# Expert results scattered to token rows as they come, read back by plain loads, with three shared tiles between the batches

## What is computed

```
nx = rmsnorm(X, g2); logits = nx @ Wr.T + expert_bias
topw, topi = top_k(softmax(logits), 2); topw = softmax(topw)
shared = swiglu(nx, sW1, sW2, sW3)
eo[e] = (silu(nx @ eW1[e].T) * (nx @ eW3[e].T)) @ eW2[e].T      # 8 experts, 256 wide
out = x + gb * (X + shared + sum over the two chosen experts of topw * eo)
```

## Time and profile before

| | us |
|---|---|
| median of 3 timed runs (1410.04 to 1413.48) | 1412.84 |
| the profiled execution, its own time | 1408.02 |
| its span, first to last instruction | 1405.9 |
| TensorE busy, share of the span | 1262.6 (90%) |
| VectorE busy | 1083.5 (77%) |
| ScalarE busy | 877.1 (62%) |
| GpSimd busy | 412.5 (29%) |
| mean granted TensorE clock | 0.966 of full |

### The profile page before, as it was taken

The page is one execution under the profiler, slowest core; times in us unless marked ns, Lnnn a source line. Parts: engine busy times, 40 slices in busy tenths (PEclk is TensorE's granted clock), DMA queues, the critical chain, the costliest instruction groups (busy, mean ns, idle before and its releaser), DMA issues.

```text
span 1405.9 us, 18718 instructions
## 1 busy us (share of the span) xinstructions
PE 1262.6 (90%) x5880; PEld 901.4 (64%) x5880; DVE 1083.5 (77%) x2304; ACT 877.1 (62%) x1399; POOL 412.5 (29%) x440
## 2 busy tenths in 40 slices
PE   3975768999999999999999999989997979989985
PEld 2434545666667666767756766656556868778874
DVE  4867768888988888888978887899755786557756
ACT  2645756767878667767797776657577634334431
POOL 0156421112211112201113211115631355853234
PEclk9988879999999999999999999999999989999998
DMA  5001036000000000000000002002212536645445
GB/s 203 8 1 60 1 120 239 9 5 5 9 4 9 4 5 5 8 5 5 8 4 9 23 12 86 16 5 79 83 53 95 172 117 192 203 136 153 146 136 162
DMA packets 64893, 91.22 MB, mean 65 GB/s; under 512 B 12703, under 2 KB 52704, under 8 KB 64544
## 3 DMA queue, kind: packets, MB, share of 16 engines
q1 hardware_dynamic: 45662, 55.27, 11.9%
q0 software_dynamic: 13920, 31.40, 8.1%
q10 hardware_dynamic: 5218, 3.39, 0.8%
HBM read 48.15 MB, written 41.80 MB: 64 GB/s over the span
## 4 chain that ended last, share of the span: by engine, by line
PE 65%; DVE 13%; ACT 8%; issue 6%; POOL 4%; DMA 2%; ACTq 1%; another core or an unknown queue 1%; POOLq 0%; DVEq 0%
PE PS L1982 10%; PE PS L1905 7%; PE PS L1908 6%; PE PS L1922 6%; PE PS L1925 6%; PE PS L1923 6%; PE PS L1857 6%; PE PS L2012 5%; DVE mx L1226 4%; DVE PL L1272 3%; PE PS L1843 2%; PE PS L1966 2%; POOL xbuf L1645 2%; PE PS L1995 1%; PE PS L1870 1%
## 5 line engine op out<-in xcount | busy, mean ns | idle before, releaser
L1226 DVE TENSOR_REDUCE mx<-PS 128x1 f32<-128x512 f32 x512 | 344.3, 684 | 48.3 <-PE PS L1857 47.2
L845 ACT ACTIVATE PT<-PS 128x1024 f32<-128x1024 f32 x256 | 262.3, 1025 | 188.6 <-PE PS L1908 182.5
L1272 DVE TENSOR_TENSOR PL<-PT,PH 128x512 fp32r<-128x512 f32 x512 | 358.7, 708 | 16.3 <-ACT PH L848 15.0
L848 ACT ACTIVATE PH<-PT 128x1024 fp32r<-128x1024 f32 x256 | 271.5, 1060 | 8.1
L1922 PE MATMUL PS<-PH,VH 128*65 128x512 f32 x512 | 213.2, 416 | 2.2 <-ACT OZ L859 2.0
L1925 PE MATMUL PS<-PL,VH 128*65 128x512 f32 x512 | 202.7, 396 | 0.0
L1923 PE MATMUL PS<-PH,VL 128*65 128x512 f32 x512 | 202.4, 395 | 0.0
L1857 PE MATMUL PS<-KA,Q 128*128 128x512 f32 x384 | 154.3, 411 | 13.5 <-DVE mx L1226 9.4
L1905 PE MATMUL PS<-Q,KA 128*128 128x512 f32 x384 | 129.8, 420 | 2.9 <-DMA Q<-mT 2.9
L1908 PE MATMUL PS<-Q,KB 65*128 65x512 f32 x384 | 122.0, 399 | 0.0
L950 ACT ACTIVATE sg<-PS 128x256 f32<-128x256 f32 x110 | 42.2, 383 | 103.0 <-PE PS L1982 86.5
(11 more groups left out here) (268 smaller groups left out, 2543.3 us busy)
## 6 DMA issues: line engine op xcount, KB each, us to landing
xbuf<-xT SPq DMA_DIRECT2D x26, 384.0 KB, 4.5
nxT<-in_wexp SPq DMA_DIRECT2D x9, 768.0 KB, 4.5
xg<-xbuf SPq DMA_DIRECT2D x52, 128.0 KB
ybuf<-nxT SPq DMA_DIRECT2D x44, 128.0 KB
ybuf<-yo SPq DMA_DIRECT2D x34, 128.0 KB
x<-in_x SPq DMA_DIRECT2D x8, 512.0 KB, 12.1
x_scratch<-x SPq DMA_DIRECT2D x2, 2048.0 KB, 7.3
nxT<-norm_scratch POOLq DMA_DIRECT2D x32, 128.0 KB
```

The source lines that it names most:

```text
L845: act.activation(PT[:, gs % 4, :], PS[:, bk:bk + 2, :].rearrange("p a n -> p (a n)"), ACT.Exp, scale=0.125).then_inc(sem("pt"), 1)
L848: act.activation(PH[:, gs % 4, :], PT[:, gs % 4, :], ACT.Copy).then_inc(sem("pt_h"), 1)
L1226: dve.tensor_reduce(mx[:, qb % 2, i, c:c + 1], PS[:, k, :], AX, ALU.max).then_inc(sem("dve_out"), 1)
L1272: dve.tensor_tensor(PL[:, gs % 4, cols], PT[:, gs % 4, cols], phf[:, gs % 4, cols], ALU.subtract).then_inc(sem("pl"), 1)
```

## The change

What a tile of experts computes is now sent straight to token order. A new buffer `ytok` in HBM has two rows of 256 per token of both batches, and behind them as many rows as there are expert rows, for those that belong to no token. So that a tile knows where its rows go, each row of `xbuf` gets two numbers more (`DR` = 258): the code is filled by a list (`nowhere`) for all rows, and `scatter` overwrites it with the token's own (`hdr`) for the rows in use. Per expert tile VectorE makes 128 row numbers `yi` from the two numbers and the tile's expert, and GpSimd stores the result with one indirect DMA, where SyncE had a plain one. `gather` becomes a plain load on SyncE's queue, 16 in all, each of two groups of 128 tokens with both rows; `y12` is now two places of twice the size. The batch 1 `scatter_load` goes to SyncE's queue. Three of the 16 closing shared tiles are moved between the batches, and the side jobs get other steps. The rows of `xbuf` are no longer contiguous for the zeroing DMAs, and a DMA of 4992 pieces of 8 bytes is added behind each batch's zeros. `NEARLY` is 3 and `FIRST` 97.

The order:

```
-TILES = ([(None, NT + i) for i in range(NT)] + [(0, i) for i in range(NTI)] + [(1, i) for i in range(NTI)]
-         + [(None, i) for i in range(NT)])
+TILES = ([(None, NT + i) for i in range(NT)] + [(0, i) for i in range(NTI)] + [(None, i) for i in range(NEARLY)]
+         + [(1, i) for i in range(NTI)]
+         + [(None, i) for i in range(NEARLY, NT)])
...
-            (20, 1, total_jobs(0)),
+            (17, 1, total_jobs(0)),
             (17, 1, route_jobs(1, 4)),
-            (30, 3, scatter_jobs(1)),
-            (50, 1, total_jobs(1)),
-            (NT + NTI + 3, 0.5, gather_jobs(0)),
-            (NT + NTI + 8, 0.5, finish_jobs(0)),
-            (NT + 2 * NTI + 1, 1, gather_jobs(1)),
-            (NT + 2 * NTI + 5, 1, finish_jobs(1))]
+            (30, 2.4, scatter_jobs(1)),
+            (56, 0.5, total_jobs(1)),
+            (NT + NTI + 9, 0.25, gather_jobs(0)),
+            (NT + NTI + 13, 0.5, finish_jobs(0)),
+            (FIRST + 2, 1, gather_jobs(1)),
+            (FIRST + 4, 2, finish_jobs(1))]
```

On SyncE:

```
+        def gather(h):
+            b, i, r = h // 8, h % 8, h % NYQ
+            for k in range(NYO):
+                w.wait_ge(sem(f"d_y{k}"), 16 * stored(b, k))
...
+            if h >= NYQ:
+                w.wait_ge(sem("comb"), 2 * (h - NYQ) + 2)
+            src = ytok[2 * b * S:2 * b * S + 2 * S, :].rearrange("(p t j) d -> p t j d", p=P, t=NT)
+            sp.dma_start(yq[:, r, :, :, :], src[:, 2 * i:2 * i + 2, :, :]).then_inc(sem(f"d_yq{r}"), 16)
...
+        def scatter_load(b, i):
+            n, r = b * NT + i, (b * NT + i) % NSX
+            if b:
+                w.wait_ge(*kept(token(b, i)))
+                w.wait_ge(sem(f"d_sx{r}"), 32 * (n // NSX))
+                sp.dma_start(sx[:, r, 0:D], nrm[b, i]).then_inc(sem(f"d_sm{r}"), 16)
...
             for n in range(NTI // 3):
-                sp.dma_start(zv[n], bc(zero, 3, 1)).then_inc(sem("d_zero"), 16)
+                sp.dma_start(rows_of[n][:, :, 0:D], bc(zero, 3, 1)).then_inc(sem("d_zero"), 16)
+            sp.dma_start(xbuf[b][:, D:DR], I["nowhere"][b]).then_inc(sem("d_zero"), 16)
```

On ScalarE's queue, at the start:

```
-        act.dma_start(thr[:, :], I["thr"]).then_inc(sem("d_route"), 16)
+        act.dma_start(thr[:, :], I["thr"].to_broadcast([P, NTI])).then_inc(sem("d_route"), 16)
+        act.dma_start(hdr[:, :, :, :], I["codes"]).then_inc(sem("d_route"), 16)
```

On VectorE, in the chooser, the placer and behind the split of tile `s`:

```
+                    mark(dve.tensor_scalar(hdr[:, b, :, 0], rm[:, 4, :], -1.0, float(NE), ALU.mult, ALU.add))
...
+            dve.tensor_scalar(texpf[:, b, :], r_v[:, :], float(NE - 1), None, ALU.min).then_inc(sem("texp"), 1)
...
+                dve.scalar_tensor_tensor(yi[:, k % NYI:k % NYI + 1], xr[r][:, D:D + 1], texpf[:, g, i:i + 1],
+                                         xr[r][:, D + 1:DR], ALU.not_equal, ALU.add).then_inc(sem("yi"), 1)
```

On GpSimd, in `scatter`, and a store per expert tile at the head of each step:

```
+            pool.tensor_copy(sx[:, r, D:DR], hdr[:, b, i, :]).then_inc(sem("sx"), 1)
+            w.wait_ge(sem("sx"), n + 1)
...
+        def store(s):
+            k, r = nth[s], nth[s] % NYO
+            w.wait_ge(sem("yo"), k + 1)
+            w.wait_ge(sem("yi"), k + 1)
+            pool.indirect_dma_start(
+                out=ytok, out_offset=bass.IndirectOffsetOnAxis(ap=yi[:, k % NYI:k % NYI + 1], axis=0),
+                in_=yr[r], in_offset=None).then_inc(sem(f"d_y{r}"), 16)
```

More of the change, by code:

```diff
@@ L29 @@
 NYO = 7
+NYI = 16
+NYQ = 2
+NEARLY = 3
+DR = D + 2
 def bc(ap, n, axis):
@@ L158, in gather_jobs @@
 def gather_jobs(b):
-    return [("gather", b * NT + i) for i in range(NT)]
+    return [("gather", b * NT // 2 + i) for i in range(NT // 2)]
 def finish_jobs(b):
@@ L309, in _build @@
     x1d = nc.dram_tensor("x1_scratch", [NB, S, D], F32, kind="Internal").ap()
-    xbuf = [nc.dram_tensor(f"xbuf{b}", [NTI * P, D], F32, kind="Internal").ap() for b in range(NB)]
-    ybuf = [nc.dram_tensor(f"ybuf{b}", [NTI * P, D], F32, kind="Internal").ap() for b in range(NB)]
+    xbuf = [nc.dram_tensor(f"xbuf{b}", [NTI * P, DR], F32, kind="Internal").ap() for b in range(NB)]
+    ytok = nc.dram_tensor("ytok", [2 * NB * (S + NTI * P), D], F32, kind="Internal").ap()
     tri = sb("tri", [P, 2, P])
@@ L434, in _build @@
     wl = sb("wl", [P, NE, 2, 768], F32R)
+    xg2 = sb("xg2", [P, NXR - 4, DR])
+    xr = [xg[:, i, :] for i in range(4)] + [xg2[:, i, :] for i in range(NXR - 4)]
+    yq = y12[:, :, :, :].rearrange("p (r t) j d -> p r t j d", r=NYQ)
     xhf = xh[:, :, :, :].bitcast(F32)
     hhf = hh[:, :, :, :].bitcast(F32)
-    sx = nxT[:, 1, 1024:2048].rearrange("p (s d) -> p s d", d=D)
+    w0 = W[0][:, :, :, :].rearrange("p a c n -> p (a c n)")
+    sx = w0[:, 3072:3072 + NSX * DR].rearrange("p (s d) -> p s d", d=DR)
     wst = nxT[:, :, :].rearrange("p c n -> p (c n)")[:, 0:4 * 768].rearrange("p (s c n) -> p s c n", s=2, c=2)
@@ L631, in fetch @@
             m = s - NT
-            experts_free(w)
-            keys_free(w)
-            pe_of(w, ("proj_last", NT - 1, 0))
+            attention_done(w)
             if m >= NXR:
                 w.wait_ge(sem("tx"), s - NXR + 1)
+                if TILES[s - NXR][0] is not None:
+                    w.wait_ge(sem("yi"), nth[s - NXR] + 1)
             if g is None:
@@ L681, in _ @@
         work = {"spill": spill, "max_turn": max_turn, "load_w": load_w, "split_down": split_down, "finish": finish,
-                "rescale": rescale}
+                "rescale": rescale, "gather": gather, "scatter_load": scatter_load}
         run(work, FRONT)
@@ L1685, in split_down @@
                                ALU.subtract).then_inc(sem("w_down"), 1)
-        def gather(n):
-            b, i, s = n // NT, n % NT, n % NG
-            experts_free(w)
-            for r in range(NYO):
-                w.wait_ge(sem(f"d_y{r}"), 16 * stored(b, r))
-            w.wait_ge(sem("w2h"), 1)
-            w.wait_ge(sem("w2l"), 1)
-            w.wait_ge(sem("tx"), NT)
-            for m in range(token(1, NT - 6), token(1, NT)):
-                w.wait_ge(*kept(m))
-            if n >= NG:
-                w.wait_ge(sem("comb"), n - NG + 1)
-            for j in range(2):
-                pool.indirect_dma_start(
-                    out=y12[:, s, j, :], out_offset=None, in_=ybuf[b],
-                    in_offset=bass.IndirectOffsetOnAxis(ap=slot[:, b, j, i:i + 1], axis=0)).then_inc(sem(f"d_pair{s}"), 16)
+        def store(s):
+            g, i = TILES[s]
+            if g is None:
+                return
+            k, r = nth[s], nth[s] % NYO
[4 more added lines that the diff above has]
+                in_=yr[r], in_offset=None).then_inc(sem(f"d_y{r}"), 16)
         after_last("zero")
@@ L1711, in _ @@
                 "q_hi": q_hi, "z_out": z_out, "z_back": z_back, "scatter": scatter, "split_down": split_down,
[L1712 removed]
+                "rl_scale": rl_scale, "scatter_load": scatter_load, "t_mul": t_mul, "t_add": t_add}
         run(work, FRONT)
@@ L1719, in _ @@
                 run(work, LOOP[gs, part])
-        for s in range(-3, NTL + 3):
+        run(work, TAIL[-3])
+        for s in range(-2, NTL + 2):
+            if 0 <= s - 2 < NTL:
+                store(s - 2)
             run(work, TAIL[s])
+        run(work, TAIL[NTL + 2])
     @block.tensor
@@ L2073 @@
     wol[:64, :D], wol[64, D] = tr(a["L0_ffn_Wo"])[3 * 64:], 1.0
+    token = 16 * np.arange(P)[:, None, None] + np.arange(16)[None, None, :] + 2048 * np.arange(2)[None, :, None]
+    codes = np.stack([np.zeros(token.shape), 2 * token], axis=3).astype(np.float32)
+    nowhere = np.zeros((2, NTI * P, 2), np.float32)
+    nowhere[:, :, 1] = 2 * 4096 + 2 * np.arange(2 * NTI * P).reshape(2, NTI * P)
     arrays = {
@@ L2082 @@
         "thr": (np.arange(NTI) * P).astype(np.float32).reshape(1, NTI), "mask": mask,
+        "codes": codes, "nowhere": nowhere,
         "pri": np.arange(NE, 0, -1).astype(np.float32),
```

97 lines of the change are left out of this document (56 added, 41 removed).

## The result

The changed kernel takes 1464.77 us (median of 4 runs, 1461.71 to 1466.31) against 1413.16 (4 runs): ratio 1.0369, 95% interval 1.0351 to 1.0387. It is slower by 51.6 us; 1409.8 was forecast, with 1394 to 1429 as the range. The profiled execution has a span of 1459.5 us, 53.6 more than before.

The account below looks back on a forecast made before the run. It took TensorE to bound the kernel outside three holes beside dense indirect DMAs, with the gathers last at the end. Terms -9.7 - 15.3 + 5 + 3 + 0.5 + 1 + 11 + 0.5 + 1 = -3.0 gave 1409.8 us, range 1394 to 1429.

Parts of the forecast that it names:

- GpSimd's queue in the batch 1 scatters: Before the first batch 1 tile: result stores between scatters delay the last scatter; TensorE's 6.0 hole becomes about 9, +3 us.
- Zeros and lists: SyncE's queue ahead of the row of maxima near 238: lists 10.6, zero rows 2, less 1.6 slack, +11 us.
- The last attention block: Before the attention's end: sixteen copies in GpSimd's queue, where projection already waits now and then, +1 us.
- the holes beside the gathers: Expert tiles beside gathers: TensorE's holes go if dense indirect DMAs make them, -15.3 us; otherwise nothing.
- two finishes in a step: Closing tiles: VectorE's step with two finishes takes 3.15 us, over TensorE's 2.54, for eight steps, +5 us.
- the end: After the last tile's start: plain loads replace gathers, leaving 9.3 us of that tile's own chain instead of 19.0, -9.7 us.
- routing and passes: Batch 1 routing and later passes: an added small VectorE operation per tile can meet GpSimd's passes, +0.5 and +1 us.
- the front: Start of the kernel: two more loads ahead on ACT's queue, +0.5 us.
- Rival 1: Front and routing: lists ride inside the slack and routing gets its relief, 9 and 4.5 us better, 1396; chance 0.33.
- Rival 2: Eighth step of the attention loop: lists cost as much per piece as whole rows, 18 us worse, 1428; chance 0.11.
- Rival 3: Expert tiles: the holes aren't the gathers' doing and stay, 15 us worse, 1425; chance 0.13.
- Rival 4: Batch 1 routing: VectorE's code operation is caught behind GpSimd's passes, 2.0 us each, eight times, 15 us worse, 1425; chance 0.11.

Follow-up runs that it names:

- e4: Changed kernel with the batch 1 token loads back on GpSimd, one plain DMA ahead of each pair of scatters: 1446.9 us, single execution.
- e5: Changed kernel with one plain GpSimd DMA of 8 bytes behind each pair of batch 1 scatters: 1441.3 us, single execution.
- h1: Token order for batch 1 alone, batch 0 keeping plain stores and gathers, three shared tiles between batches: 1409.8 us (kernel before beside it: 1406.3).
- e6: Changed kernel with a GpSimd memset of 128x512 behind each pair of batch 1 scatters: 1451.6 us, single execution.
- e8: Changed kernel without the 32 GpSimd copies of codes; one DMA per batch writes them behind the kept rows: 1450.8 us, single execution.
- e9: Changed kernel with a plain GpSimd DMA of 8 bytes behind every second pair of batch 1 scatters only: 1448.9 us, single execution.
- e3: Changed kernel with zeros and lists issued one at every second attention step from step 12: 1437.9 us, single execution.
- e1: Changed kernel with both lists issued at attention steps 12 and 20, behind the row of maxima; zeros stay in place: 1445.0 us, single execution.
- e2: Changed kernel with zeroing DMAs writing whole rows of 258 numbers, no lists, and result stores skipping rows without a token: 1446.0 us, single execution.
- e7: Kernel before with one plain GpSimd DMA of 8 bytes behind each pair of gathers, 32 in all: 1407.8 us, single execution.
- e10: Kernel before with a GpSimd memset of 0.54 us behind each pair of gathers: 1398.9 us in a single execution; timed again, ratio 0.9928.

## Why the prediction was wrong, step by step

**The step that failed** is "GpSimd's queue in the batch 1 scatters", +3, with 6 less to 16 more as its bounds; it measured **+25.6**. It went wrong twice. The first error: the prediction had read that the holes of before stand beside dense indirect DMAs, took 15.3 us off for that, and then filled the batch 1 scatters with 49 indirect DMAs where there were 32, with the loads that had spaced them taken away, and charged only their time on the queue. It put nothing down for new holes. e4 and e5, which space the same DMAs again, take 92.4 and 93.2 us for tiles 30 to 58 instead of 102.6, so the holes are some 10 us of the 25.6.

The second error was in the queue time itself, and by e4 and e5 it is the other 15. The last scatter was put 67.6 us after 1168.85, as if the first could start as early as before. It started 10.1 us after tile 30 instead of 3.7, because stores that wait for their results stand ahead of it, and the last one ends 84.1 us after tile 30 instead of 53.9. In the changed kernel pauses of over 0.6 us in GpSimd's queue add up to 11.4 us on the way, against 2.2 before; but e4 has no such pause, does the loads as well, and ends at 83.8. With the stores of batch 0 out of this queue (h1) the last scatter ends at 57.4, and the whole loss is gone. The wait of 6.4 us for the first batch 1 tile never came in the changed kernel, since TensorE arrived later than the data; e4, with few holes, shows it at 12.5.

**Zeros and lists**, +11, measured 28.5 in the profiled run. The place was right (SyncE's queue ahead of the row for the ninth step) and so was the lack of slack. The zeros were mis-sized: 2 us with 7 as their upper end, measured 10.5. In the six profiled kernels with the lists ahead of the row (after, e4, e5, e6, e8, e9) the delay at step 10, less what was there at step 3, is 19.9 to 28.5, median 21.9 (e3, with nothing ahead of the row, shows 1.6 by the same count). Less the 10.5 of e1, the lists cost 9.4 to 18.0, median 11.4, or 18 ns a piece, where 10.6 and 17 ns were taken, and the execution of the changed kernel that stands here is the dearest of the six.

What the trace shows is 26 DMAs of the same 1 KB pieces in 34.1 us at a pitch of 1032 bytes and in 28.9 at 1024, 18% more; the row behind them lands 4 us later after its issue as well.

The Trainium skill, DMA: Bandwidth & Descriptors, How a descriptor splits into AXI transactions, says of reads that a transaction covers at most 256 bytes and has to start at a multiple of 256, so that a piece which starts elsewhere begins with a partly used one. For 1 KB that makes five transactions instead of four; an estimate by their number is up to 25% more, 36 us. e1 (34.1) and e2 (36.0) agree in size, but these are writes, and no run here shows the transactions themselves.

The prediction also weighed a rule of the same page of the Trainium skill (Specifications), that pieces below 512 bytes are read, modified and written; by its estimate the lists would cost 14.2 us at least. The 9.4 to 18.0 measured, with 11.4 as the median, do not decide that.

**The last attention block**, +1, measured 9.2, some 5 of it the copies (e8). The copies were priced by their duration, but each stands in the queue of the four small DMAs that the projection waits for. In the changed kernel TensorE waits 6.64 and 3.77 us there, where the kernel before waits 2.83 and 0.83, and e8 4.22 and 2.74:

```profile
1023.47 0.37 PE L1916 MATMUL PS<-ident,m 128*4 128x128 f32 x1 [6.64 <-DVE m L1263]
...
1067.21 1.22 PE L1923 MATMUL PS<-woa,O 128*128 128x256 f32 x2 [3.77 <-POOL O L1671]
```

**Right in mechanism and size:** the holes beside the gathers, -15.3 (tiles 58 to 109: -7.9, after the finishes' 4.5 and two steps at tiles 72 and 74 that are 2.4 longer, since the first operation of a finish, beside one of GpSimd's passes, takes 2.03 us instead of 0.47); two finishes in a step, +5 (five steps of 3.10 to 4.06 us, 4.1, and 0.4 at the last tile). **Right in direction:** the end, -9.7, measured -7.4 (11.6 us behind the last tile's start, not 9.3: the last two pairs of finishes stand between that tile's splits); routing and passes, +1.5, measured 2.1 from tile 1 to 30; the front, +0.5, measured 1.8, which is within what kernels that are alike there differ by.

**The rivals.** Rival 1 (the lists ride inside the slack) fell at the attention loop's ninth step, 28.7 us late. Rival 2 (dear lists) named the right queue and step and gave 1428, but its cause fell: the lists cost 18 ns a piece, and it was the zeros that were dear. Rival 3 (the holes stay) fell: they went with the gathers, and e7 and e10 show what brings them and takes them away. Rival 4 fell as a price, though its mechanism is there: ten of the 78 code operations run beside one of GpSimd's passes and take 1.1 to 3.1 us instead of 0.21, the longest 3.12 at 1166.69, but tiles 1 to 30 lose only 2.1 us in all, and the steps from 58 to 71 keep 2.55 us. No rival said that the holes would move to where the indirect DMAs move, and the 1429 at the top of the range had no room for it.

## What to carry to other kernels

Price an indirect DMA by its neighbours as well as by its own 1.26 us: in this kernel the other engines stood still for microseconds at a time when GpSimd issued 0.75 to 0.79 of them a microsecond, at 0.65 to 0.69 mostly less, and a spacing of 0.4 us per pair of gathers cost less than it gave. When a mechanism explains a stall of the kernel before, run the same mechanism over every stretch that the change makes denser. Large writes whose date doesn't matter go behind the small transfer that an engine waits for, and a row pitch of 1032 bytes in place of 1024 is paid on every row (34.1 us of issue against 28.9).

## What the hardware showed that was not expected

The spacing itself: 0.79 indirect DMAs a microsecond give holes of up to 4.5 us in the kernel before, 0.69 holes of 1.1 at most (e10), and what fills the space, GpSimd's own work or a DMA, hardly matters beside the gathers; between scatters and stores the DMA helped more (93.2 against 98.9 us). In a hole TensorE's signals come late. At 1225.8 in the changed kernel the signals of two down products, an up product and two turns arrive within 0.25 us, after 3.6 us without any, though an up product alone takes 1.4; one of VectorE's came on time meanwhile, at 1223.1. In this hole, then, it is the report of TensorE's work that is held back, not the work. By what, no run here tells: the silences of TensorE's signals end at no fixed point of GpSimd's instructions, and no instruction fetch falls into that hole (the nearest starts at 1226.9).

A plain DMA issued by GpSimd takes it 0.57 us for 8 bytes as for 128 KB. An indirect one takes 0.96 whether its rows have 1024 or 1032 bytes.
